# A DLRM tower: each sample's gram as a matmul of its own, 26 columns by 26, in place of four samples at once

## The reference

```python
e = jnp.stack([tbl_0[ids[:, 0]], ..., tbl_26[ids[:, 26]]], axis=1)      # (2048, 27, 128)
dot_products = jnp.einsum('bnd,bmd->bnm', e, e)
r, c = np.tril_indices(27, k=-1)
z = dot_products[:, c, r]                                               # (2048, 351)
h = jnp.concatenate([z, dense_ctx], axis=1)                             # (2048, 367)
h = jnp.maximum(h @ W_top1 + b_top1, 0.0)                               # 512 wide
h = jnp.maximum(h @ W_top2 + b_top2, 0.0)                               # 256 wide
y = h @ W_top3
```

## Time and profile before

| | us |
|---|---|
| median of 3 runs | 418.44 |
| lowest and highest | 417.51, 419.03 |
| the profiled execution | 416.94 |
| its span, first to last instruction | 415.0 |
| PE busy, share of the span | 368.2, 89% |
| POOL busy | 279.3, 67% |
| DVE busy | 280.8, 68% |
| ACT busy | 191.4, 46% |
| mean granted TensorE clock | 0.979 |

### The profile page before, as it was taken

How to read it: one execution, slowest core, us unless ns; L and a number is a source line. 1 busy time by engine, 2 the same in 40 slices (tenths; PEclk the granted TensorE clock), 3 DMA queues, 4 the chain that set the end, 5 groups by cost and what they waited for, 6 DMA issues and landing times.

```text
span 415.0 us, 7809 instructions
## 1 busy us (share of the span) xinstructions
PE 368.2 (89%) x2856; PEld 351.5 (85%) x2856; DVE 280.8 (68%) x588; ACT 191.4 (46%) x562; POOL 279.3 (67%) x295
## 2 busy tenths in 40 slices
PE   0843799999899999999999999999999999989857
PEld 0743699998899998999899988999899988989756
DVE  5737987888757866697658865696668774732551
ACT  2260545645544554545454554554444554444331
POOL 6777877777777777777777777777777777740000
PEclk9995999999999999999999999999999999999997
DMA  7984283332323332332423232332423231110000
GB/s 185 241 209 124 78 217 106 90 89 69 92 68 82 84 83 65 82 86 67 93 66 94 76 79 69 89 78 70 89 76 90 64 86 51 52 41 0 2 1 1
DMA packets 23969, 35.11 MB, mean 85 GB/s; under 512 B 7936, under 2 KB 17832, under 8 KB 23932
## 3 DMA queue, kind: packets, MB, share of 16 engines
q0 software_dynamic: 9216, 18.89, 20.0%
q1 hardware_dynamic: 14716, 15.73, 13.7%
HBM read 34.59 MB, written 0.01 MB: 83 GB/s over the span
## 4 chain that ended last, share of the span: by engine, by line
PE 74%; DVE 11%; DMA 5%; issue 4%; SPq 3%; ACT 2%; DVEq 0%
PE e_banks L425 30%; PE g_banks L459 25%; PE e_banks L437 6%; PE w_bank L500 6%; PE w_bank L489 5%; DMA ids_wide<-in_ids 5%; DVE zt L575 4%; DVE h L253 3%; DVE one_hot L563 3%; SPq L349 2%; PE w_bank L478 1%; ACT et L272 1%; PE e_banks L459 1%; SPq L339 1%; ACT hT L252 1%
## 5 line engine op out<-in xcount | busy, mean ns | idle before, releaser
L396 POOL DMA_INDIRECT rows<-in_tbl,idx x288 | 278.6, 967 | 88.7 <-issue 86.0
L563 DVE TENSOR_TENSOR one_hot<-ids_wide,row_no 125x1024 fp32r<-125x1024 int32 x144 | 168.6, 1216 | 41.4 <-PE e_banks L425 30.6
L425 PE MATMUL e_banks<-one_hot,table_hi 125*128 125x256 f32 x576 | 150.6, 298 | 27.3 <-DVE table_lo L554 23.5
L425 PE MATMUL e_banks<-one_hot,table_lo 125*128 125x256 f32 x576 | 144.5, 287 | 0.0
L425 PEld LDWEIGHTS e_banks<-one_hot,table_hi 125*128 125x128 f32 x576 | 112.8, 196 | 28.9 <-issue 28.9
L459 PE MATMUL g_banks<-et 128*122 128x104 f32 x992 | 115.2, 268 | 1.4 <-issue 0.7
L459 PEld LDWEIGHTS g_banks<-et 128*122 128x122 f32 x992 | 111.0, 187 | 2.6 <-issue 1.9
L425 PEld LDWEIGHTS e_banks<-one_hot,table_lo 125*128 125x128 f32 x576 | 113.0, 196 | 0.0
L252 ACT ACTIVATE z<-g_banks 26x208 f32<-26x208 f32 x184 | 61.7, 336 | 67.1 <-PE g_banks L459 64.1
L272 ACT ACTIVATE et<-e_banks 128x256 f32<-128x256 f32 x72 | 45.0, 626 | 72.8 <-PE e_banks L425 72.8
L263 ACT ACTIVATE et<-e_banks 128x512 f32<-128x512 f32 (+1 forms) x96 | 51.6, 555 | 21.3 <-PE e_banks L437 20.9
(11 more groups left out here) (26 smaller groups left out, 85.5 us busy)
## 6 DMA issues: line engine op xcount, KB each, us to landing
ids_wide<-in_ids SPq DMA_DIRECT2D x72, 125.0 KB
rows<-in_tbl,idx POOLq DMA_INDIRECT x288
et<-in_tbl SPq DMA_DIRECT2D x9, 448.0 KB
w<-in_W_top SPq DMA_DIRECT2D x2, 256.0 KB
w<-in_W_top SPq DMA_DIRECT2D x1, 512.0 KB
et<-in_tbl SPq DMA_DIRECT2D x9, 52.0 KB
w<-in_W_top SPq DMA_DIRECT2D x1, 222.0 KB
idx<-in_idx SPq DMA_DIRECT2D x1, 202.5 KB, 2.6
```

The source lines that it names most:

```text
L396: pool.indirect_dma_start(rows[:, k % RING, a, :], None, tables[f], bass.IndirectOffsetOnAxis(ap=idx[:, t, f:f + 1], axis=0)).then_inc(row ...
L425: last = nc.tensor.matmul(e_bank[n % E_BANKS][:, 0:UNIT], part[:, q, c, :], one_hot[:, hot_slot(o, piece), c % PIECE, :], start=(c == 0 an ...
L563: nc.vector.tensor_tensor(one_hot[:, hot_slot(o, piece), :, :], ids_wide[:, o % IDS_RING, :].unsqueeze(1).broadcast_to([OP, PIECE, UNIT]), ...
```

## The change

Each sample gets its own float32 matmul: 26 weight columns, 26 moving columns, written to partitions 32g to 32g+25 of one bank. The program gives such a matmul the array's tile of 128 rows x 32 columns, at column 0, 32, 64 or 96 by the sample's g; all other matmuls keep the whole array. Four G steps a tile remain, with 32 matmuls each. Two steps fill one bank (16 strips of 26 columns, on four groups of partitions), and after every second step ACT alone copies the whole bank, 128 partitions x 416, into `z`. DVE copies no grams. There are two semaphores, `g_filled` and `g_drained`, that count half tiles; TensorE waits only before the first step of a half, for the copy of the same half of the tile before. The zeroing of `z` and of the places in `et` gives way to one zeroing of `g_banks`. The use of `e_banks` in the last tile goes.

```diff
-    GW = QUADS * NP
-    GROWS = (QUADS - 1) * STRIP + NP
-    G_HALF = 4
-    G_PIECES = STRIP // (2 * G_HALF)
+    G_PIECES = 4
+    G_STEP = STRIP // G_PIECES
+    G_BANK = STRIP // 2
...
-        def drain_grams(me, engine, s):
+        def drain_grams(act, s):
             _, t, p = s
-            engine.wait_ge(g_filled, G_PIECES * t + p + 1)
-            if p == 0 and t >= PAIR and me == "act":
-                engine.wait_ge(z_turned, 2 * (t - PAIR + 1))
-            for g in range(QUADS):
-                if g_engine(t, g) != me:
-                    continue
-                strip = slice(g * STRIP, g * STRIP + NP)
-                src = gram_banks(t, p)[strip, :, 0:G_HALF * GW].rearrange("p k (s c) -> p k s c", c=GW)
-                out = z[strip, t % PAIR, 2 * G_HALF * p:2 * G_HALF * (p + 1), :]
-                copy(me, out.rearrange("p (k s) n -> p k s n", s=G_HALF), src[:, :, :, g * NP:(g + 1) * NP]
-                     ).then_inc(g_drained[g], 1)
+            half = p // 2
+            act.wait_ge(g_filled, 2 * t + half + 1)
+            if half == 0 and t >= PAIR:
+                act.wait_ge(z_turned, 2 * (t - PAIR + 1))
+            nc.scalar.activation(z[:, t % PAIR, G_BANK * half:G_BANK * (half + 1), :],
+                                 g_banks[:, half, 0:G_BANK * NP].rearrange("p (s n) -> p s n", n=NP), ACT.Copy
+                                 ).then_inc(g_drained, 1)
...
-                banks = gram_banks(t, p)
-                for i in range(2 * G_HALF):
-                    b = (2 * G_HALF * p + i) * QUADS
-                    four = et[:, t % ET_TILES, b:b + QUADS, :]
-                    last = nc.tensor.matmul(banks[0:GROWS, i // G_HALF, i % G_HALF * GW:(i % G_HALF + 1) * GW],
-                                            four.rearrange("p g f -> p (g f)")[:, 0:GROWS], four[:, :, 1:NF],
-                                            start=True, stop=True)
-                last.then_inc(g_filled, 1)
+                half = p // 2
+                if t > 0 and p % 2 == 0:
+
+                    pe.wait_ge(g_drained, 2 * (t - 1) + half + 1)
+                for i in range(G_STEP):
+                    at = (G_STEP * p + i) % G_BANK * NP
+                    for g in range(QUADS):
+                        sample = et[:, t % ET_TILES, (G_STEP * p + i) * QUADS + g, :]
+                        last = nc.tensor.matmul(g_banks[g * STRIP:g * STRIP + NP, half, at:at + NP],
+                                                sample[:, 0:NP], sample[:, 1:NF], start=True, stop=True)
+                if p % 2 == 1:
+                    last.then_inc(g_filled, 1)
...
-            nc.vector.memset(z[:], 0.0).then_inc(pads_ready, 1)
-            nc.vector.memset(et[:, 0:2, :, NF:STRIP], 0.0).then_inc(pads_ready, 1)
+            nc.vector.memset(g_banks[:], 0.0).then_inc(g_banks_zeroed, 1)
...
-                    if o == NOH - 1:
-                        dve.wait_ge(lo_ready, NOH)
-                        nc.vector.memset(et[:, 2:4, :, NF:STRIP], 0.0).then_inc(pads_ready, 1)
-                elif s[0] == "G":
-                    drain_grams("dve", dve, s)
```

More of the change, by code:

```diff
@@ L49, in dlrm_tower @@
     NP = NF - 1
-    GW = QUADS * NP
-    GROWS = (QUADS - 1) * STRIP + NP
-    G_HALF = 4
-    G_PIECES = STRIP // (2 * G_HALF)
-    assert G_HALF * GW <= BANK
+    G_PIECES = 4
+    G_STEP = STRIP // G_PIECES
+    G_BANK = STRIP // 2
+    assert G_BANK * NP <= BANK and G_BANK == 2 * G_STEP
     M1 = N1 // P
@@ L206, in dlrm_tower @@
         ids_wide_in = [sem(f"ids_wide_in{i}") for i in range(IDS_RING)]
-        pads_ready = sem("pads_ready")
+        g_banks_zeroed = sem("g_banks_zeroed")
         table_in = [sem(f"table_in{q}") for q in range(NOH)]
@@ L216, in dlrm_tower @@
         g_filled = sem("g_filled")
-        g_drained = [sem(f"g_drained{q}") for q in range(QUADS)]
+        g_drained = sem("g_drained")
         z_turned = sem("z_turned")
@@ L232, in rows_landed @@
             return 16 * sum(len(FEATS[c % CHUNKS]) for c in range(k % RING, k + 1, RING))
-        def gram_banks(t, p):
-            return e_banks[:, 0:2, :] if t == LAST_TILE and p % 2 == 1 else g_banks[:]
         def hot_slot(o, piece):
             return (PIECES * o + piece) % HOT_RING
-        def g_engine(t, g):
-            return "act" if g < (2 if t == LAST_TILE else 3) else "dve"
         def w_engine(s):
@@ L446, in grams @@
                 if t == 0 and p == 0:
[L447 to L452, removed]
-                    for g in range(QUADS):
-                        pe.wait_ge(g_drained[g], before + 1)
-                banks = gram_banks(t, p)
-                for i in range(2 * G_HALF):
-                    b = (2 * G_HALF * p + i) * QUADS
-                    four = et[:, t % ET_TILES, b:b + QUADS, :]
-                    last = nc.tensor.matmul(banks[0:GROWS, i // G_HALF, i % G_HALF * GW:(i % G_HALF + 1) * GW],
-                                            four.rearrange("p g f -> p (g f)")[:, 0:GROWS], four[:, :, 1:NF],
-                                            start=True, stop=True)
-                last.then_inc(g_filled, 1)
+                    pe.wait_ge(g_banks_zeroed, 1)
+                half = p // 2
[3 more added lines that the diff above has]
+                    at = (G_STEP * p + i) % G_BANK * NP
+                    for g in range(QUADS):
+                        sample = et[:, t % ET_TILES, (G_STEP * p + i) * QUADS + g, :]
[3 more added lines that the diff above has]
+                    last.then_inc(g_filled, 1)
             def wait_packed(t, c):
@@ L540, in _ @@
                     drain_look_up(act, s)
-                elif s[0] == "G":
-                    drain_grams("act", act, s)
+                elif s[0] == "G" and s[2] % 2 == 1:
+                    drain_grams(act, s)
                 elif s[0] == "pack":
@@ L569, in turn_tile @@
             def turn_tile(t):
-                for g in range(QUADS):
-                    dve.wait_ge(g_drained[g], G_PIECES * (t + 1))
+                dve.wait_ge(g_drained, 2 * (t + 1))
                 if t >= PAIR:
```

## The result

| | before | after |
|---|---|---|
| median, us | 417.98 (4 runs, 416.75 to 419.03) | 397.62 (4 runs, 396.33 to 398.58) |
| profiled execution, its span | 416.94, 415.0 | 396.33, 394.4 |
| ratio | | 0.951 (95%: 0.947 to 0.955) |

The kernel became 4.9% faster, where 442 us, slower, was forecast. It is the rival "the strips work side by side", with the gathers as the next bound.

A forecast was written before the change was run, and what follows sets the result against it. The prediction took TensorE as the bound, with POOL's gathers close beneath. It summed 416.9 + 6.5 (grams) + 19.8 (strip borders) - 0.8 (drains) = 442.4 us, with a range from 392 to 515 us.

The forecast's parts named there:

- the strips work side by side: Rival at the gram matmuls: four strips overlap, grams shrink from 108 us to 30 to 60, time 395 us; chance 0.24.
- What bounds the kernel now: Whole kernel: TensorE is the bound in the steady part, so a G step's added or saved cost is felt in full.
- The second limit: POOL's 288 gathers: a faster TensorE can pull the last transposes forward by some 20 us and no further.
- The gram matmuls: G steps on TensorE: 4,096 records at 28 ns make 114.7 us against 108.2, a term of +6.5 us.
- the forecast's bounds: Cost of one gram record: 22.5 ns in proportion to weight columns, 35 ns by a line through two full-array shapes.
- its wide upper one: Cost of one gram record: as much as today's shortest, 105.6 ns, so 324 us more for the grams; chance 0.05.
- Going in and out of the strips: Borders of the gram stretches on TensorE: overlap lost, 61 x 2 x 0.162 = +19.8 us, bounds 0 and 31.
- The drains: Copies of grams by ACT and DVE: nothing in the steady part, waits and the end together -0.8 us.
- Start and instruction stream: Zeroing at the start and transfer of 6,144 more instruction records: 0 us.
- The clock: Rival at the G stretches: the granted clock falls to half, grams take 229 us, time 558 us; chance 0.06.
- no overlap of load and matmul: Rival at the gram records: load and matmul one behind the other, 44.5 ns, time 510 us; with a fixed part, chance 0.21.
- The rival's own sum: End of the run with strips side by side, bound by the gathers: 393 us, with slack at the ring 395.

The follow-up runs named there:

- f2: The kernel before, with POOL gathering only two rows of features a chunk from the 13th chunk on; 417.87 us, ratio 1.000 to before.
- e1: The changed kernel with every sample's gram written to the one strip at column 0; 431.63 us in one run, before on the same chip 419.39.
- g2: The changed kernel with fewer gathers, a tile's second and fourth G step pulled forward to the first and third; 372.07 us, ratio 0.890 to before.
- g3: The changed kernel with fewer gathers, grams drained as before the change, ACT three strips and DVE one; 382.33 us, ratio 0.918 to before.
- f4: The changed kernel with a ring of eight chunks and an L2 step between the last tile's second and third G step; 394.99 us, ratio 0.946.
- g1: f1 once more, unchanged, as reference for g2 and g3 on one chip; 379.60 us, ratio 0.908 to before.
- f1: The changed kernel with only two rows of features gathered a chunk from the 13th chunk on; 378.71 us, ratio 0.906 to before.
- f3: The changed kernel with a gather ring of eight chunks in place of six, et without its unused places; 395.89 us, ratio 0.948 to before.

## Why the prediction was wrong

**What bounds the kernel now: right.** f2 shows it: 108 gathers gone, ratio 1.000. The second limit was read rightly too. It was put for the last transposes, "some 20 us and no further", and these moved by 17.8. That the medians differ by 20.4 is in part luck: 2.8 us come from the shorter tail, while the last chunk was turned 5.06 us after its last gather was done, where 2 had been allowed.

**The gram matmuls: the step that failed.** "A G step is ... 64 records ... I take 28 ns" lets the 4,096 records follow one another. For one strip that was right (e1: 27 ns). But the four samples of a group go to four strips, and there a record starts every 8.6 ns. By the ledger TensorE's grams cost 49.4 us less (118.7 - 69.3) with 10 us of dearer borders in it, so this term was about -59 us, not +6.5. Neither of the forecast's bounds, 22.5 and 35 ns, nor its wide upper one, held this; all three were drawn from rows of the whole array, where the question cannot arise. The rival had it, and the text even knew its condition, "it decides once the mean pace is below some 20 ns". What misled me was the row that I set against it: PEld busy in 46.41 of 50 us. That busy loader says nothing about loads that go to different strips: a load of 26 columns lasts 103 ns by its record, and with a start every 8.6 ns twelve such records lie over one another.

The Trainium skill, "TensorE: Matmul & The Clock Gate", Part 3, gives 2.38 times for three column strips at 512 columns. The trace agrees: four strips at 26 columns give 27 / 8.6 = 3.1 times, and in the first half of a step, where most starts are 6 to 7 ns apart, about four times. The Trainium skill, "TensorE: Matmul & The Clock Gate", Part 1, "Wait — 56ns, not 53.3ns?", says that start-to-start never drops below about 25 ns however small the matmul. e1's 27 ns agree with that for one strip; across strips the Trainium skill and the 8.6 ns differ, and the measurement decides. The chance of 0.24 was too low: the diff places neighbours in four strips, and the only reason against it was the busy loader.

**Going in and out of the strips: right in kind.** The rule of the Trainium skill, "TensorEngine Tiling (Array Packing)", Key Properties, that a change of tiling mode drains the engine, agrees with the trace in that both ways are dearer: 94 ns more going in and 71 coming out, 61 times. The records do not show an engine that is quite empty: the last transposes end 0.07 us after the first gram starts (200.71 + 0.60 against 201.24), by a modelled end. Of the 19.8 us forecast the records show 10.1 (61 x 0.165), about half; the term put 162 ns on each side. (g2's 0.27 us is another quantity, the whole way in and out, of which before had its share too.) In the kernel as it is the borders cost less than that, since PE waits 22.4 us for rows anyway.

**The drains: right.** 0.4 us at the end, by the chain: from the last gram (380.13) to the turn (380.70) 0.57 us with a copy of 0.53. In the steady part nothing that g3 could show.

**Start and instruction stream: wrong.** "0 while a block comes in less time than it lasts." In after the last tile's 256 matmul records have a hole of 2.06 us, of which f4 removes most in the trace, and where TensorE waits for no rows (g1) the holes make about 20 of 54 us of gram stretches (a step without them is 0.55 us, 64 are 35). The 2.06 us stand around one packet of the instruction queue; here the DMA view of after, 375 to 380 us (tenths and GB/s in 40 slices, then the queue):

```profile
DMA  0000000000000000040000000000000000000000
GB/s 0 0 0 0 0 0 0 0 0 0 0 0 0 0 0 0 0 131 0 0 0 0 0 0 0 0 0 0 0 0 0 0 0 0 0 0 0 0 0 0
...
q8 instruction: 1, 0.02, 1.1%
```

It is the only transfer in these 5 us, from 377.2 to 378.1, and TensorE stops from 377.55 to 379.61. In f1, g1, g2, g3 and f3 the hole stands at the same record, the 221st of the 256. That the small holes have the same source is not shown: of g1's 82 only 10 fall on a packet, 12%, and packets are under way in 14% of the time.

**The clock, and no overlap of load and matmul: no part on the chip of after.** The granted clock is 1.00 from 200 to 250 us in after as before, and without overlap a gram record would have had to start 44 ns behind the last, where even e1's start after 27:

```profile
200.00:250.00 50.00, 43.74 (x830) 38.66 (x828) 33.36 (x67) 19.51 (x53) 37.80 (x41) 1.00 0.34 79
```

**The rival's own sum** was 368.8 + 2 + 23.6 - 3 + 1.9 = 393, called 395 (368.8 is where the last gather is done, not where it is issued). Measured, term by term: the last gather is done at 368.55, its chunk is turned 5.06 us later, the tail is 20.8, and 1.9 around: 396.3. The last chunk does not wait for its rows but for PE. The gathers hold the chain until 342 us; from 345 to 373.6 PE is busy in 27.8 of 28.6 us, with the look-ups and layers that stand ahead of the last chunk in its order. So in that stretch the other bound is back.

## What to carry to other kernels

Where a change sends neighbouring matmuls to different strips of 32 or 64 columns, price them by the strip, not by the record: here the pace on one strip divided by about three for four strips, provided that the program alternates between strips. Only matmuls of 26 by 26 and pairs of 58 by 52 were measured. Then look for the second bound at once; half of TensorE's 40 to 50 us went to gathers that stood ready beneath. And with four times as many instructions pauses appear that no wait explains, about 0.3 us a step where TensorE is the bound. Fewer borders pay (7.5 us for 28). Whether it pays to part long runs of tiny matmuls by a large one is not shown: g2's longer runs lost nothing, and f4's 0.9 us lie within the intervals.

## What I had not expected of the hardware

- In four strips, load and matmul of 26 columns each start every 8.6 ns (6 to 7 in the first half of a step, about 10 behind it) while by its record one load lasts 103 ns and one matmul 191 ns; in one strip every 27 ns.
- The order decides it: the same matmuls strip by strip take 23 ns each.
- At the pace of 8.6 ns, and not at 27 ns, TensorE pauses behind some 45 matmul records for 0.1 to 0.4 us a step, and once for 2.06 us in 256 records.
- A whole way into the strips and out again costs 0.28 us by the start times, 0.27 by g2.
- On one chip these holes were 0.5 us after every handful of records, the granted clock fell to 0.50 behind them, and the kernel before took 537 us instead of 418.
